# Moving SyncE's bulk transfers in a decoder layer: store, x, contexts and masks go behind the self-attention stack

## The reference, cut to what matters

```python
x = x + attn(layernorm(x))                    # 16 heads of 8, bias from w_rel, softmax over 128 keys
x = x + xattn(layernorm(x), ctx, ctx, mask)   # 16 heads of 8, keys and values from ctx, mask per key
x = x + ffn(layernorm(x))                     # 128 -> 512 gate and up, silu(gate) * up, -> 128
```

## Time and profile before

| what | value |
|---|---|
| median of 3 runs | 456.83 us (456.45 to 457.15) |
| the profiled execution | 452.96 us |
| its span, first to last instruction | 451.1 us |
| time outside the span | 452.96 - 451.1 = 1.9 us |
| TensorE matmul busy | 385.8 us, 86% |
| VectorE busy | 381.2 us, 85% |
| ScalarE busy | 346.4 us, 77% |
| GpSimd busy | 308.2 us, 68% |
| queue q1, share of 16 DMA engines | 54.6% |
| mean granted TensorE clock | 0.967 of full speed |

### The profile page before, as it was taken

The page is one execution under the profiler, slowest core; times in us unless marked ns, Lnnn a source line. Parts: engine busy times, 40 slices in busy tenths (PEclk is TensorE's granted clock), DMA queues, the critical chain, the costliest instruction groups (busy, mean ns, idle before and its releaser), DMA issues. The chain is left out here.

```text
span 451.1 us, 16947 instructions
## 1 busy us (share of the span) xinstructions
PE 385.8 (86%) x5436; PEld 312.2 (69%) x5468; DVE 381.2 (85%) x1922; ACT 346.4 (77%) x962; POOL 308.2 (68%) x783
## 2 busy tenths in 40 slices
PE   3348878999999999999989999999999999866662
PEld 2236667778887888788878887888778877544541
DVE  4954757789999999999989998999999999787643
ACT  2125676889998999999988998999889988775441
POOL 6554586878777778778876777778778766565120
PEclk9998998999999999999999999999999999998885
DMA  6576476666667566756676657576766553323000
GB/s 195 147 186 170 107 218 169 178 157 175 175 160 199 150 180 157 197 155 177 156 183 138 184 155 186 156 179 150 193 160 167 166 146 90 87 78 102 8 6 12
DMA packets 100171, 67.19 MB, mean 149 GB/s; under 512 B 73269, under 2 KB 90421, under 8 KB 100085
## 3 DMA queue, kind: packets, MB, share of 16 engines
q1 hardware_dynamic: 98209, 64.08, 54.6%
q10 hardware_dynamic: 1876, 2.03, 1.4%
HBM read 46.08 MB, written 19.07 MB: 144 GB/s over the span
## 5 line engine op out<-in xcount | busy, mean ns | idle before, releaser
L976 DVE CUSTOM_DVE_ANT_0 biased<-bank,mask_bias 128x128 bf16<-128x128 f32 x512 | 114.9, 285 | 13.0 <-PE bank L1245 12.8
L981 DVE TENSOR_REDUCE neg_max_S<-bank 128x4 f32<-128x512 f32 x128 | 87.4, 684 | 16.3 <-PE bank L1245 15.5
L664 ACT ACTIVATE probs_X<-bank 128x512 f32<-128x512 f32 x128 | 71.6, 586 | 13.4 <-PE bank L1263 12.8
L664 ACT ACTIVATE probs_S<-bank 128x512 f32<-128x512 f32 x128 | 75.1, 593 | 8.4 <-PE bank L1263 7.8
L1245 PE MATMUL bank<-stack_k_S,stack_q_S 120*128 120x128 bf16 x512 | 52.0, 226 | 6.1 <-DMA stack_k_S<-scratch_S 5.0
L1245 PE MATMUL bank<-stack_k_X,stack_q_X 72*128 72x128 bf16 x512 | 49.9, 221 | 7.3 <-DMA stack_k_X<-scratch_X 6.1
L1263 PEld LDWEIGHTS bank<-stack_q_X,stack_k_X 74*128 74x128 bf16 x512 | 40.5, 99 | 16.3 <-issue 1.6
L1263 PE MATMUL bank<-stack_q_X,stack_k_X 74*128 74x128 bf16 x512 | 50.7, 222 | 0.0
L1260 PE MATMUL bank<-ident_bf,mask_bias 128*128 128x512 bf16 x128 | 50.1, 392 | 0.0
L1263 PE MATMUL bank<-stack_q_S,stack_k_S 122*128 122x128 bf16 x512 | 47.4, 224 | 2.5 <-DMA stack_q_S<-neg_maxT_S 1.9
L1245 PEld LDWEIGHTS bank<-stack_k_S,stack_q_S 120*128 120x128 bf16 x512 | 40.7, 104 | 8.5 <-issue 5.8
(11 more groups left out here) (165 smaller groups left out, 1120.9 us busy)
## 6 DMA issues: line engine op xcount, KB each, us to landing
stack_q_S<-scratch_S SPq DMA_DIRECT2D x32, 288.0 KB
stack_k_S<-scratch_S SPq DMA_DIRECT2D x32, 288.0 KB
stack_q_X<-scratch_X SPq DMA_DIRECT2D x32, 288.0 KB
stack_k_X<-scratch_X SPq DMA_DIRECT2D x32, 288.0 KB
scratch_S<-qk_parts_S SPq DMA_DIRECT2D x32, 192.0 KB, 3.0
scratch_X<-qk_parts_X SPq DMA_DIRECT2D x32, 192.0 KB, 2.5
ctxT<-ctx SPq DMA_DIRECT2D x8, 256.0 KB, 3.0
scratch_S<-qk_parts_S SPq DMA_DIRECT2D x32, 64.0 KB, 2.6
```

The lines of the kernel that those rows point to most:

```text
L664: act.activation(probs[a][:, b % 2, c, :], bank_b[c % 2][:, :], ACT.Exp).then_inc(sems["exp_" + a], 1)
L976: last = dve.tensor_tensor_reduce(biased[:, c, hh, :], quarter(bank_a[c % 2], hh), mask_bias[:, b % 2, :], -1.0, -2.0 * BIG, ALU.add, ALU.min,
L981: dve.tensor_reduce(neg_max[a][:, first_head(c):first_head(c) + 2 * HC - 1:2], bank_a[c % 2][:, :].rearrange("i (h j) -> i h j", h=HC), AX ...
```

## The change

SyncE's list is reordered; no other engine's list changes, and no transfer is added or removed. In `ramp` and `step` the calls of `load_x`, `store` and `load_c` stand behind `stack_in("S")` now, just ahead of `parts_again("X")`. `fill` and `drain` are as they were.

```diff
             def ramp(st):
                 max_in("S", st, 1)
                 parts_out("X", st, 1)
-                load_x(st, -1)
-                store(st, 14)
-                parts_again("S", st, -1)
-                load_c(st, 0)
-                parts_out("S", st, -1)
-                stack_in("X", st, 1)
-                max_in("X", st, 2)
-                stack_in("S", st, -1)
-                parts_again("X", st, 0)
-
-            def step(st):
-                store(st, 5)
-                parts_out("X", st, 1)
-                max_in("S", st, 1)
-                load_x(st, -1)
-                load_c(st, -1)
                 parts_again("S", st, -1)
                 parts_out("S", st, -1)
                 stack_in("X", st, 1)
                 max_in("X", st, 2)
                 stack_in("S", st, -1)
+                load_x(st, -1)
+                store(st, 14)
+                load_c(st, 0)
+                parts_again("X", st, 0)
+
+            def step(st):
+                parts_out("X", st, 1)
+                max_in("S", st, 1)
+                parts_again("S", st, -1)
+                parts_out("S", st, -1)
+                stack_in("X", st, 1)
+                max_in("X", st, 2)
+                stack_in("S", st, -1)
+                store(st, 5)
+                load_x(st, -1)
+                load_c(st, -1)
                 parts_again("X", st, 0)
```

## The result

| | median | runs |
|---|---|---|
| before | 456.03 us | 22 |
| changed | 457.90 us | 22 |
| ratio changed / before | 1.0064 (95%: 1.0041 to 1.0086) | |

What follows compares the result with a forecast made beforehand. TensorE (97% busy) and VectorE (96%) bound the steady part, chains of latencies the ramp. 452.96 + 6.0 + 0.5 - 2.5 = 456.96 us, plus 3.87 up to the median, gave 460.8 us, slower by 0.9%; range 454.5 to 467.5.

Steps and rivals of the forecast that it cites:

- x comes late in the ramp: Ramp: groups 4 and 5 of x, issued behind the S stack, make VectorE wait; first X maximum 6.7 us late.
- 73.7: Ramp: forecast start in us of VectorE's first X maximum, 67.05 before the change.
- the lower bound: Ramp, group 4 of x: with an empty queue it lands 3.0 us behind its issue, at 59.3 us.
- the mask's 5.3: Fill: a mask load right behind an S stack took 5.3 us to land; by it group 4 lands at 61.6.
- +6.0 and +0.5 us: Ramp: 6.7 us of delay less 0.7 made good gives +6.0; TensorE's clock falling while it idles gives +0.5.
- The store's 1.0 us: Steady part: a store step, its store ahead of the parts of X, costs the X chain about 1.0 us.
- So some 0.6 of the 1.0 us is lost again: Steady part: 512 KB ahead of X's parts delay them; 0.4 us stay in each of six store steps, -2.5 us.
- the sign of a faster queue: Steady part: batch 7 to batch 27 in below 226 us, where 230.2 was measured before and about 228 foreseen.
- +6.5 - 2.5 = +4.0: Whole kernel: ramp +6.0 and clock +0.5, less 2.5 in the steady part, take 452.96 to 456.96 us.
- The choke: Rival, steady part: 512 KB ahead of the parts cost 1.3 us net in seven store steps; 472.4 us, half 467.8; chance 0.12.
- The draw: Rival: ramp loses only group 4's 4.0 us, second wait falls into idle time, steady part gives 4; 456.8 us; chance 0.17.
- the faster case: Rival: the ramp makes its delay good, only the steady gain stays; 453.8 us; chance 0.18.

Runs made afterwards that it cites:

- the kernel that kept the clock up: Ramp alone changed, plus groups of 16 unread matmuls in ramp steps 2 and 3 that also wait for `exp_S`; 1.0155 against before, 462.95 us against 462.17 without them.
- at 1 MB: Steady step alone changed, plus two unread 256 KB loads behind store and contexts in each store step; 1.0105 against before, 2.1% slower than without the extra loads.
- group 5 alone: Kernel before with only group 5 of x moved behind the S stack of ramp step 1, group 4 and steady step as before; ratio 1.0140.

## Why the prediction was right, point by point

- **x comes late in the ramp: shown.** Foreseen were waits of 5.2 and 4.2 us, measured 4.38 and 4.14; the first X maximum at 73.7, measured 73.65. Putting `load_x` back removes the loss.
- **How well 73.7 was hit is luck.** SyncE issued group 4 at 55.15, earlier than the 56.3 foreseen, and it landed 4.1 us later (59.3), the lower bound rather than the mask's 5.3. So the reciprocal of attention sums started 60.38 - 58.17 = 2.2 us late, not 4.0. The scores of batch 3 were as late as foreseen all the same (66.26, foreseen 66.2), since half clock behind the stall added 2.2 us, which the prediction had not put there (it had 0.5 us for the clock in all). The two errors cancelled. The same ramp gave 76.92 and 76.32 in two other profiles, again with 1.91 us for the four matmuls behind the stall. Both loads landed 4.1 us behind their issue; that lies nearer to the 3.4 us of the median x load of before than to the 5.3 us of the mask, so most of the lateness of group 4 is its late issue (5.5 us), and little of it the stack's bytes.
- **+6.0 and +0.5 us: right within what the runs can tell.** The ramp alone costs 1.6%, 7.2 us (mean of two kernels), and both intervals hold the 6.5 foreseen. The clock's share is not settled: half clock lengthened TensorE's work behind the first stall by 2.2 us, but the kernel that kept the clock up was no faster.
- **The store's 1.0 us: somewhat too small.** It was read from one step. Over five store steps the X stack went out 6.4 us behind the first part on average, 1.3 us more than the 5.07 of a step without bulk. The store alone gives 3.2 of the 4.9 us.
- **"So some 0.6 of the 1.0 us is lost again": wrong.** This is the step that failed. The sum let the 512 KB begin behind the landing of the S stack and pass at 229 GB/s, so that the bulk was through 8.1 us behind the stack's issue and the parts at 8.8 to 9.3 us. Measured in x = 12 were 6.6 and 7.4 us: the bulk moved together with the end of the stack, in a queue that reached 282 GB/s. Of the 1.5 us by which the bulk came early, the higher rate accounts for some 0.4 us (524,288 B at 282 instead of 229 GB/s), the overlap for the rest. The trace of before already had 285 GB/s, in the stretch of the X stack shown above. The gain is 4.9 us instead of 2.5, and the 20 steps took 225.73 us, below the 226 that the prediction named as the sign of a faster queue. By the Trainium skill, "DMA: Bandwidth & Descriptors", "Bandwidth", with its 358 GB/s, nothing would be lost, and the steady part would give 6 us, as an estimate. The measured rate lies between the two, and the gain nearer to the page's.
- **The sum: right in sign, and in size by errors that cancel in part.** +6.5 - 2.5 = +4.0 foreseen, +7.2 - 4.9 = +2.3 by the two halves, +2.9 measured on the whole.
- **The rivals.** The choke needs more than 512 KB in a row; at 1 MB it is there. The draw and the faster case fall with the ramp: the second wait did not fall into idle time (group 5 alone costs 1.4%), and the delay is not made good, as batch 7 is 6.65 us late, after a first X maximum that was 6.60 us late.

## What to carry to other kernels

Before a load is moved back in an issue list, compare its landing with its first use, not with its place: in the ramp two loads had 2.1 and 1.2 us to spare and were moved by more than 5. Behind a transfer that waits, a load inherits the wait and the bytes. The same move can pay in the steady part and cost in the ramp, so split the edit by stage and measure each half. And where transfers stand in a row, don't add the landing time of the first to the moving time of the next: here they overlapped.

## What the runs showed of the hardware that was not expected

- One queue moved 282 GB/s for 4.5 us where stack, store, contexts and parts stood in it in a row, and 285 GB/s in 1.5 us of a stack before the change, against 229 while the store moved. With the setting in and the end of the burst the mean over 6 us was 235.
- TensorE idle for 3.8 us came back at half clock: four matmuls of 128x512 took 1.91 us instead of 1.03. The granted clock in that stretch was 0.70.
- Executions of one and the same kernel spread over 3% (449 to 465 us over 28 runs of before), more than any effect here.
